# Scores of two heads in row halves, turned weights copied by two engines, and a distance of five units in the second wide attention

## The reference, cut to what matters

```python
h = layernorm(X)                                   # 16 sequences x 256 x 128
q, k, v = split(h @ W_qkv + b_qkv)                 # 16 heads of 64
s = q @ k.T * 64 ** -0.5 + slope[head] * (j - i)   # causal: -inf where j > i
o = softmax(s) @ v
X = X + (concat(o) @ W_out + b_out)
```

## Time and profile before

| | us |
|---|---|
| median of 3 runs | 4947.14 |
| lowest, highest | 4945.99, 4955.91 |
| the profiled execution | 4966.88 |
| its span, first to last instruction | 4965.2 |
| scores of `wb_`, first to last start | 1038.6 to 1653.1 |

### The profile page before, as it was taken

How to read it: one execution, slowest core, us unless ns; L and a number is a source line. 1 busy time by engine, 2 the same in 40 slices (tenths; PEclk the granted TensorE clock), 3 DMA queues, 4 the chain that set the end, 5 groups by cost and what they waited for, 6 DMA issues and landing times. The chain is left out here.

```text
span 4965.2 us, 90774 instructions
## 1 busy us (share of the span) xinstructions
PE 3830.9 (77%) x25840; PEld 2716.8 (55%) x25840; DVE 3461.7 (70%) x9524; ACT 2340.5 (47%) x5537; POOL 2387.3 (48%) x3900
## 2 busy tenths in 40 slices
PE   7889797679999799568868936568775887799365
PEld 5666565656666466456646626523332665466265
DVE  7788676656666676566658856669998664588566
ACT  3444464356656466234446624345553454366243
POOL 4666442534444443446643245367776662232443
PEclk9999898789999899689989959879998999899598
DMA  6000232100000132133323211212221330132113
GB/s 233 0 0 0 100 123 85 52 22 1 0 0 0 68 124 97 37 125 106 106 81 122 102 36 46 69 52 64 62 62 64 115 114 27 58 122 102 36 46 86
DMA packets 244547, 341.24 MB, mean 69 GB/s; under 512 B 26976, under 2 KB 187120, under 8 KB 243120
## 3 DMA queue, kind: packets, MB, share of 16 engines
q1 hardware_dynamic: 230960, 309.19, 18.7%
q0 software_dynamic: 13184, 27.22, 1.6%
HBM read 182.77 MB, written 147.26 MB: 66 GB/s over the span
## 5 line engine op out<-in xcount | busy, mean ns | idle before, releaser
L522 DVE TENSOR_REDUCE l0att_rowmax<-l0att_S 128x2 f32<-128x512 f32 x512 | 339.3, 685 | 128.1 <-PE l0att_S L701 126.0
L892 POOL TENSOR_TENSOR wb_prob<-wb_prob,wb_rden 128x128 f32<-128x128 f32 (+1 forms) x512 | 248.2, 506 | 360.9 <-DVE wb_rden L1069 360.6
L522 DVE TENSOR_REDUCE l1ffn_rowmax<-l1ffn_S 128x2 f32<-128x512 f32 x512 | 337.4, 685 | 88.8 <-PE l1ffn_S L701 85.7
L1982 POOL TENSOR_TENSOR ssm_hc<-core_AW_all,ssm_Cs 128x512 f32<-128x512 f32 x256 | 320.9, 1270 | 130.4 <-DVE core_AW_all L2128 95.9
L1433 POOL DMA_INDIRECT results<-e_y,e_back x220 | 213.8, 972 | 291.0 <-DVE e_y L1661 262.3
L934 ACT ACTIVATE wb_prob<-wb_biased,wb_nmax 128x128 f32<-128x128 f32 (+1 forms) x512 | 228.6, 447 | 236.1 <-DVE wb_nmax L1062 233.7
L2227 PE MATMUL ssm_Y<-ssm_hc,core_ident 128*128 128x512 f32 x512 | 288.5, 676 | 58.1 <-POOL ssm_hc L1982 32.3
L2128 DVE TENSOR_TENSOR_SCAN core_AW_all<-core_AW_all,ssm_U 128x512 f32<-128x512 f32 x256 | 310.1, 1212 | 1.4 <-ACT core_AW_all L2071 1.4
L701 PE MATMUL l1ffn_S<-l1ffn_K,l1ffn_Q 128*128 128x512 f32 x512 | 250.0, 492 | 77.5 <-DVE l1ffn_rowmax L522 43.2
L1774 PE MATMUL e_H<-e_xT,e_W1s 128*128 128x128 f32 x1760 | 250.4, 286 | 71.9 <-issue 48.2
L701 PE MATMUL l0att_S<-l0att_K,l0att_Q 128*128 128x512 f32 x512 | 249.0, 490 | 61.7 <-DMA l0att_K<-bounce 49.0
(11 more groups left out here) (498 smaller groups left out, 11482.2 us busy)
## 6 DMA issues: line engine op xcount, KB each, us to landing
bounce<-l0att_parts SPq DMA_DIRECT2D x128, 256.0 KB, 2.8
bounce<-l1ffn_parts SPq DMA_DIRECT2D x128, 256.0 KB, 2.8
ssm_Cs<-c_rows SPq DMA_DIRECT2D x128, 256.0 KB, 3.1
routed<-core_Y SPq DMA_DIRECT2D x8, 2048.0 KB, 25.4
l0att_Q<-bounce SPq DMA_DIRECT2D x128, 128.0 KB
l0att_K<-bounce SPq DMA_DIRECT2D x128, 128.0 KB
bounce<-l1att_parts SPq DMA_DIRECT2D x64, 256.0 KB, 2.8
l1ffn_Q<-bounce SPq DMA_DIRECT2D x128, 128.0 KB
```

The source lines that it names most:

```text
L522: dve.tensor_reduce(out=rowmax[:, jp, qt, 2 * pair:2 * pair + 2], in_=S[a % 2][:].rearrange("p (j k) -> p j k", j=2)[:, :, 0:keys(qt)], op ...
L892: ins = pool.tensor_tensor(out=prob[:, w_ % 4, a:b], in0=prob[:, w_ % 4, a:b], in1=rden[:, w_ % 4, n:n + 1].to_broadcast([P, b - a]), op=A ...
L1982: pool.tensor_tensor(out=hc[:, u % 4], in0=hs[:, u % 4], in1=Cs[:, n % 4], op=ALU.mult)\
```

## The change

Only `wb_` is changed:

- `score` runs once in two units and makes the scores of both heads, head 0 from rows 0 to 63 of q and k into one bank, head 1 from rows 64 to 127 into the other. It waits for both maxima of the pair before.
- k is kept once, without zeros; the clearing goes, and its evacuation is one activation of 128 rows.
- The copies of the turned weights alternate: the even units of a turn are copied by ScalarE, after its exponentials, the odd ones by VectorE.
- `LAG` goes from 3 to 5; the buffers of probabilities and their statistics go from 4 to 8 (`NP`).

```diff
-    LAG = 2 if HS == 1 else 3
+    LAG = 2 if HS == 1 else 5
+    NP = 4 if HS == 1 else 8
     YT_AT, OUT_AT = LAG + 3, LAG + 4
...
-        kT = sb("kT", [P, SLOTS, HS, GN])
+        kT = sb("kT", [P, SLOTS, GN])
...
-        prob = sb("prob", [P, 4, WIDE])
-        probT = sb("probT", [P, 4, WIDE])
+        prob = sb("prob", [P, NP, WIDE])
+        probT = sb("probT", [P, NP, WIDE])
...
-                    for j in range(HS):
-                        rows = slice(j * DH, (j + 1) * DH)
-                        ins = act.activation(kT[rows, m % SLOTS, j, :], bank("k", m)[rows, :], ACT.Identity,
-                                             bias=bk[rows, m % STEPS:m % STEPS + 1])
-                    ins.then_inc(taken["k"].sem, 1)
+                    act.activation(kT[:, m % SLOTS, :], bank("k", m)[:], ACT.Identity,
+                                   bias=bk[:, m % STEPS:m % STEPS + 1]).then_inc(taken["k"].sem, 1)
...
                 for w_ in range(UNITS):
                     exponentials(i, w_)
-                    if merged and not (first and w_ < LAG):
+                    if (merged or (w_ - LAG) % HS == 0) and not (first and w_ < LAG):
                         copy_turned(i, w_ - LAG)
...
-            if HS == 2:
-                dve.memset(kT[:], 0.0).then_inc(k_zeroed.sem, 1)
...
-                    if not merged and not (first and w_ < LAG):
+                    if not merged and (w_ - LAG) % HS == 1 and not (first and w_ < LAG):
                         copy_turned(i, w_ - LAG)
...
-                pe.wait_ge(maxed.sem, maxed.at(i, w_ - 1))
+                pe.wait_ge(maxed.sem, maxed.at(i, w_ + HS - 2))
                 for t, (a, b) in enumerate(parts):
-                    ins = pe.matmul(S[w_ % 2][:, a:b], qT[:, m % SLOTS, s * L + t * P:s * L + (t + 1) * P],
-                                    kT[:, m % SLOTS, j, s * L:s * L + b - a], start=True, stop=True)
-                ins.then_inc(scored.sem, 1)
+                    for h in range(HS):
+                        rows = slice(h * DH, (h + 1) * DH)
+                        ins = pe.matmul(S[(w_ + h) % 2][:, a:b],
+                                        qT[rows, m % SLOTS, s * L + t * P:s * L + (t + 1) * P],
+                                        kT[rows, m % SLOTS, s * L:s * L + b - a], start=True, stop=True)
+                        if t == QT - 1:
+                            ins.then_inc(scored.sem, 1)
...
                 for w_ in range(UNITS):
-                    score(i, w_)
+                    if w_ % HS == 0:
+                        score(i, w_)
```

More of the change, by code:

```diff
@@ L823, in wide_attention @@
         o_copied = sig("o_copied", 2, 2)
-        exped = sig("exped", UNITS, 4)
+        exped = sig("exped", UNITS, NP)
         inverted = sig("inverted", UNITS)
         divided = sig("divided", UNITS)
-        turned = sig("turned", UNITS, 4)
-        turn_copied = sig("turn_copied", UNITS, 4)
+        turned = sig("turned", UNITS, NP)
+        turn_copied = sig("turn_copied", UNITS, NP)
         pv_done = sig("pv_done", UNITS, SLOTS * US)
@@ L891, in turn @@
                     for n, (a, b) in enumerate(parts):
-                        ins = pool.tensor_tensor(out=prob[:, w_ % 4, a:b], in0=prob[:, w_ % 4, a:b],
-                                                 in1=rden[:, w_ % 4, n:n + 1].to_broadcast([P, b - a]), op=ALU.mult)
+                        ins = pool.tensor_tensor(out=prob[:, w_ % NP, a:b], in0=prob[:, w_ % NP, a:b],
+                                                 in1=rden[:, w_ % NP, n:n + 1].to_broadcast([P, b - a]), op=ALU.mult)
                     ins.then_inc(divided.sem, 1)
@@ L907, in _ @@
                 act.sem_inc(g.sem, g.lead)
-            if HS == 2:
-                act.wait_ge(k_zeroed.sem, 1)
             def front_h(i, s):
@@ L931, in exponentials @@
                 act.wait_ge(maxed.sem, maxed.at(i, w_ + 1))
-                act.wait_ge(turned.sem, turned.at(i, w_ - 3))
+                act.wait_ge(turned.sem, turned.at(i, w_ + 1 - NP))
                 for n, (a, b) in enumerate(parts):
-                    ins = act.activation(prob[:, w_ % 4, a:b], biased[:, w_ % 2, a:b], ACT.Exp, scale=-1.0,
-                                         bias=nmax[:, w_ % 4, n:n + 1], accum_out=total[:, w_ % 4, n:n + 1])
+                    ins = act.activation(prob[:, w_ % NP, a:b], biased[:, w_ % 2, a:b], ACT.Exp, scale=-1.0,
+                                         bias=nmax[:, w_ % NP, n:n + 1], accum_out=total[:, w_ % NP, n:n + 1])
                 ins.then_inc(exped.sem, 1)
@@ L959, in copy_turned @@
                 act.wait_ge(turned.sem, turned.at(i, w_ + 1))
-                act.wait_ge(pv_done.sem, pv_done.at(i, w_ - 3))
-                act.activation(probT[:, w_ % 4, :], T[:, 0:WIDE], ACT.Copy).then_inc(turn_copied.sem, 1)
+                act.wait_ge(pv_done.sem, pv_done.at(i, w_ + 1 - NP))
+                act.activation(probT[:, w_ % NP, :], T[:, 0:WIDE], ACT.Copy).then_inc(turn_copied.sem, 1)
             def turn(i, first, last):
@@ L997, in _ @@
                 for w_ in range(UNITS, UNITS + LAG + 2):
+                    if w_ < UNITS + LAG and (w_ - LAG) % HS == 0:
+                        copy_turned(TURNS - 1, w_ - LAG)
                     copy_out(TURNS - 1, w_)
@@ L1117, in _ @@
                 for w_ in range(UNITS, UNITS + LAG):
-                    copy_turned(TURNS - 1, w_ - LAG)
+                    if (w_ - LAG) % HS == 1:
+                        copy_turned(TURNS - 1, w_ - LAG)
             tail(TURNS - 1, 0)
@@ L1186, in weigh @@
                     opens, ends = m % STEPS == 0, m % STEPS == STEPS - 1
-                    pe.matmul(O[s][:, 0:L], V[:, m % SLOTS, s * QT, :], probT[:, w_ % 4, 0:L], start=opens, stop=False,
+                    pe.matmul(O[s][:, 0:L], V[:, m % SLOTS, s * QT, :], probT[:, w_ % NP, 0:L], start=opens, stop=False,
                               skip_group_check=True)
-                    pe.matmul(O[s][:, P:L], V[:, m % SLOTS, s * QT + 1, :], probT[:, w_ % 4, L:WIDE], start=False,
+                    pe.matmul(O[s][:, P:L], V[:, m % SLOTS, s * QT + 1, :], probT[:, w_ % NP, L:WIDE], start=False,
                               stop=ends, skip_group_check=True).then_inc(pv_done.sem, 1)
@@ L1198, in weigh @@
                         ins = pe.matmul(out, V[:, m % SLOTS, s * QT + t, h * DH:(h + 1) * DH],
-                                        probT[:, u % 4, t * L:L + t * P], start=t == 0, stop=t == QT - 1)
+                                        probT[:, u % NP, t * L:L + t * P], start=t == 0, stop=t == QT - 1)
                         if t == QT - 1:
```

20 lines of the change are left out of this document (9 added, 11 removed).

## The result

The changed kernel takes **4980.89 us** (median of 4 runs, 4974.47 to 4983.32), the kernel before 4949.66 us (4 runs on the same chip, 4945.99 to 4955.91). The ratio is 1.0053, 95% interval 1.0041 to 1.0065: slower, by 26 us (20 to 32) by that ratio, 31 by the medians. The profiled execution took 4978.69 us with a span of 4977.0; the one before 4966.88 and 4965.2. Only 12 us lie between these two executions, as the one before lies 17 us above its median. That surplus is not in this stage: the rest of the span took 4317.2 us before and 4305.0 after. So I read the stage alone, by which I mean the time from the last update of X by the block ahead to its own last update of X. It took 648.0 us before and 672.0 after, **+24.0**.

The account below looks back on a forecast made before the run. TensorE was taken to set the second wide attention's 9.40 us step. Steps +19.2, transposes -3.0, clearing -3.4 and drain +2.5 gave +15.3 us on the 4947.1 us median: 4962 us, range 4941 to 4991.

Parts of the forecast that it names:

- Row halves run together, a pair takes one head's time: TensorE's scores: two heads side by side take 0.65 us instead of 1.30, removing 1.30 us from a step.
- serial-load: Rival on score pairs: the halves' weight loads go one after another, 0.97 us a pair, result 4986 us; chance 0.10.
- no-overlap: Rival on score pairs: the row halves do not overlap, 1.05 us more a step, result 5029 us; chance 0.04.
- a pair over 0.8 us: Sign in TensorE's timeline that the prediction is wrong: a score pair's slot above 0.8 us, where 0.76 was expected.
- A change of shape costs 0.2 us each way: TensorE switching between full rows and row halves: seven switches a step instead of four, 0.6 us back.
- The free-switch rival: Rival on TensorE's shape switches: full rows and row halves count as one shape, result 4946 us; chance 0.11.
- The waits, +0.30 us a step: TensorE waiting for maxima and turned copies: 1.02 us of waits outweigh 0.7 gained; 64 steps add 19.2 us.
- The once-a-turn statistics on VectorE are waited for before and after, no change: VectorE's statistics, once a turn of the second wide attention: waited for in both kernels, so no change.
- The tail's transposes: Four transposes on TensorE, once a turn, now stand ahead of a pair that waits for VectorE: -3.0 us.
- The clearing of k, -3.4: Clearing of k, first on VectorE with ScalarE waiting, 3.47 us: it goes, counted as -3.4 us.
- Two more units drain, +2.5: End of the second wide attention: two more units drain, a turn and its copy every 1.27 us, +2.5 us.
- The faster rival: Rival on the steady step: waits do not arise, TensorE stays the bound at 8.7 us, about 4900 us; chance 0.16.

Follow-up runs that it names:

- the new order: Row-half scores, one copying engine, three units, VectorE's turns written out, v/output projection ahead of odd units' turns, ScalarE's copy-out before exponentials: 4900.76 us, 0.9882 of the kernel before.
- the two straight kernels: Changed kernel and kernel before, each with VectorE's six middle turns of the second wide attention written out: 4961.32 us (ratio 1.0012) and ratio 1.0005.
- one copier: Changed kernel, VectorE's turns written out, all turned copies on VectorE: 4952.62 us with five units from scores to turn, 4961.20 us with three units and four buffers.
- two copiers: Changed kernel, VectorE's turns written out, turned copies on ScalarE and VectorE: 4961.32 us with five units from scores to turn, 4962.1 us with three.
- the pairs: Row-half scores alone on the kernel before, VectorE's turns written out, copies on VectorE, three units, four buffers: 4961.20 us, ratio 1.0014.

## Why the prediction was right, and where it was not

4962 us was predicted, in a range of 4941 to 4991, with 0.68 on slower. Measured were 4980.9 and slower. **The mechanism that was forecast is there, but it makes the smaller part of the loss. That the kernel came out clearly slower, and near the forecast, is in good part luck:** two errors of 14 us each, in opposite directions, cancel. With VectorE's loop written out, what is left of the change is 6 us slower (0.12%, interval 0.03 to 0.20), which the prediction's own line of 0.2% counts as no change. The smaller terms below make most of what still lies between the forecast's +15.3 us and the stage's +24.0.

- *Row halves run together, a pair takes one head's time.* Right. The scores' starts in the trace are 6 to 7 ns apart, loads too, and a pair's slot is 0.86 us to the next turn, 0.84 predicted with the emptying. By the share of the ideal that the Trainium skill (TensorE: Matmul & The Clock Gate, Measured speedup vs the span model) gives for four row tiles, a pair would have been 0.85 us without its changes of shape; the forecast had 0.65, and 0.65 was measured, so two row tiles lost nothing here. The serial-load and no-overlap rivals fell with it. The prediction's own sign of being wrong, a pair over 0.8 us, was badly set: its layout already had the turn at 0.84.
- *A change of shape costs 0.2 us each way.* Right for the way in: from v's last matmul (slot 0.11) to the first score 0.20 us, so 0.10 of emptying, and 0.10 more until the second score. The way out is 0.15: from the last score to the turn 0.09 more than its slot, and 0.05 more until the turn's second matmul. The free-switch rival fell. TensorE's own step, 8.7 us in the prediction, comes to 8.67 when the two late turns (0.27 and 0.54 us, below) are taken from 9.48. It is 8.39 in the new order, where weighing goes straight into scores in both halves.
- *The waits, +0.30 us a step.* The term that was mis-sized: the step grew by **0.08**. Two of the three waits are where I put them: the second turn of pair A is 0.27 us late for VectorE's copy (0.3 predicted), the first turn of pair B 0.54 us for ScalarE's (0.56). The third, 0.16 us of pair B's scores for the maxima, did not arise: they start 0.80 us after the weighing, right behind it. I had let VectorE's next maximum start at the end of q's evacuation, 0.74 us; it starts 0.67 behind its start, and that evacuation itself starts 0.05 earlier than laid out:

```profile
1346.27 0.75 DVE L1042 TENSOR_SCALAR wb_qT<-wb_F,core_bqk 128x512 f32<-128x512 f32 x1
1346.94 0.28 DVE L1058 CUSTOM_DVE_ANT_0 wb_biased<-wb_S,wb_added 128x128 f32<-128x128 f32 x1
```

So pair B's scores come at 3.66 instead of 3.80, ScalarE's copy ends at 5.00 (predicted 5.13), the turn behind it starts at 5.05 (5.20), and the next pair at 9.48 (9.64). Besides I took the step's growth against a layout of 9.34 where 9.40 had been measured, 0.06 more. 64 x 0.22 = 14 us too much.
- *"The once-a-turn statistics on VectorE are waited for before and after, no change", and no word on the loop.* The term that was missing, put at nothing without a reason: VectorE's branch. The loop's form makes +14.7 us by the two straight kernels, and moving the loop takes off 12.4. The branch was 0.3 us before and hidden; I never asked what a change of code length does to it. Part of it is the clock, 1.3 to 1.4 us in each of two turns (13.0 and 13.1 instead of 11.65), though I had left the granted clock at 1.00.
- *The third step of a turn.* 12.46 us against 11.6 to 11.7 before, while the second fell from 9.84 to 9.57. With five units the finished output is added to X in unit 9, between statistics (8) and normalizing (10), on VectorE; before in unit 7, a step earlier. I had left this at 0; beyond the steady step it is some 0.35 us a turn. But in straight code both kernels spend 2.4 us a turn beyond the steady step here (11.86 after; 11.34 and 9.84 before), so the 0.35 belongs to the loop's form and is part of the 14.7. With one copier the straight kernels show 12.38 at five units and 11.3 to 11.7 at three, with two copiers 11.86 and 11.6 to 11.8. The tail's transposes, whose hiding I had put at -3.0 us, do leave the second step (9.84 to 9.48 in straight code), but the third grows by as much beyond the steady step, so no gain is left.
- *The clearing of k, -3.4.* Measured -4.2 from the block ahead to the first score.
- *Two more units drain, +2.5.* Measured +4.4: with one copier and five units against three 16.8 - 13.3 = 3.5, the pairs 1.0 (13.3 against 12.3), the second copier 0 to 0.7.
- *The faster rival (no waits, about 4900).* It did not come, in part for the reason given against it: ScalarE's copy behind the exponentials. VectorE's copies alone still hold the step at 9.25 us. Its 8.7 us a step exist all the same, and 4900 is what the kernel reached once the order, and not a second engine, took the waits away. The Trainium skill's advice (TensorEngine Tiling (Array Packing), PSUM Bottleneck) to empty such banks by both engines cost 0.23 us a step here, because of where the copy stands in ScalarE's queue.

## What to carry to other kernels

When a change makes the bounding engine's work shorter, lay out what it then stands in front of: here the 0.7 us a step saved on TensorE were lost to two copies that ended 1.5 and 2.6 us after their turn's start, with 1.2 and 2.1 us of TensorE's work to cover them. They were won back not by more engines or buffers but by moving other work of the same engine into the gap, and by taking the one copy that this exposed out from behind longer work. A helping engine helps only as early as its queue lets it. And with loops on the engines, read the idle time across the loop's end, before and after: here a label of "issue" there, at every pass, was a cost of where the code lay, which the change had moved without touching what the loop does at its end. To tell the two apart, move the loop or write it out, in both kernels.

## What the runs showed of the hardware

- A taken branch on VectorE cost 0.3 us or 2.8 us in this kernel, at every pass the same; 64 instructions put ahead of the loop turned the one into the other with the body unchanged. The branches of the other engines stayed at 0 to 0.33 us in all versions.
- Two matmuls in row halves of 64 start 6 to 7 ns apart and take no longer than one with 128 rows: of 272 to 383 ns, whichever the form. Entering them after full rows costs 0.10 us of emptying and 0.10 us of uncovered load, leaving them 0.09 us of emptying and 0.05 more until the second matmul.
- Going from column halves straight to row halves (weighing to scores) costs one change, not two: the score starts 0.80 us after the weighing, as a projection does in the earlier trace rows.
- After gaps of 2.3 to 2.4 us TensorE's granted clock fell in two of five passes (0.87 over one of these steps), not in the other three of the same length. It also fell behind one of six gaps of 1.5 us. The kernel before, with no gap over 1.0 us in its loop, had no fall in this stage.
